# The last layer's window, re-ordered: scores by head pairs, one other use per group, loads ahead of stores

## The reference

```python
def _L3_attn_ref(x, W_qkv, b_qkv, W_proj, b_proj):
    qkv = (x @ W_qkv + b_qkv).reshape(b, n, H, D, 3)
    q, k, v = ...                                   # 4 heads, D = 8
    scores = jnp.einsum('bhnd,bhmd->bhnm', q, k) * scale
    att = jax.nn.softmax(scores, axis=-1)
    out = jnp.einsum('bhnm,bhmd->bhnd', att, v)
    return out @ W_proj + b_proj
def _L3_ffn_ref(x, router_w, router_b, expert_w, expert_b):
    router_probs = jax.nn.softmax(x @ router_w + router_b, axis=-1)
    top_p, top_i = jax.lax.top_k(router_probs, 2)
    top_p = top_p / jnp.sum(top_p, axis=-1, keepdims=True)
    expert_out = jnp.einsum('bnd,edc->bnec', x, expert_w) + expert_b
    return jnp.einsum('bnk,bnkc->bnc', top_p, gathered)
...
t = t + _L3_attn_ref(_ln_t(t), ...)
t = t + _L3_ffn_ref(_ln_t(t), ...)
```

## Time and profile before

| | us |
|---|---|
| three executions | 8492.71, 8477.82, 8460.32 |
| profiled execution: time / span | 8467.15 / 8464.8 |
| PE busy | 6645.8 (79%) |
| DVE busy | 5057.2 (60%) |
| ACT busy | 5212.4 (62%) |
| POOL busy | 2198.2 (26%) |
| DVE peak reductions, 2048 of them | 2445.8, with 825.8 idle ahead of them |
| ACT exponentials of this layer, 4096 of them | 2214.2, with 734.9 idle ahead of them |

### The profile page before, as it was taken

One profiled execution on the slowest core, in us unless ns is written; L12 is line 12 of the kernel. 1 busy time (PEld: TensorE's weight loads), 2 busy tenths in 40 slices (PEclk: granted clock), 3 DMA queues, 4 the chain that ended last, 5 costly groups with the idle time before them and its releaser, 6 DMA issues. The chain is left out here.

```text
span 8464.8 us, 152843 instructions
## 1 busy us (share of the span) xinstructions
PE 6645.8 (79%) x48081; PEld 2768.6 (33%) x48272; DVE 5057.2 (60%) x7798; ACT 5212.4 (62%) x8588; POOL 2198.2 (26%) x3329
## 2 busy tenths in 40 slices
PE   3457888888888888666648888888888888888887
PEld 3223444444444444334432222222222222222222
DVE  5544555555555555423327777777777777777775
ACT  0116777877877787500006776776767767777676
POOL 0021222222222222200012333333333333333333
PEclk7668998899999999855658999999999999999999
DMA  1010000000000000111110000000000000000000
GB/s 70 11 40 9 5 6 6 6 5 6 6 5 6 6 6 5 17 20 20 20 16 5 7 7 9 7 9 7 7 9 7 7 9 7 9 7 7 9 7 7
DMA packets 502054, 92.38 MB, mean 11 GB/s; under 512 B 475742, under 2 KB 501295, under 8 KB 501423
## 3 DMA queue, kind: packets, MB, share of 16 engines
q1 hardware_dynamic: 500399, 86.02, 5.6%
q10 hardware_dynamic: 1152, 0.05, 0.0%
HBM read 52.47 MB, written 33.56 MB: 10 GB/s over the span
## 5 line engine op out<-in xcount | busy, mean ns | idle before, releaser
L2014 DVE TENSOR_REDUCE d_peaks<-d_p_k 128x2 f32<-128x1024 f32 x2048 | 2445.8, 1220 | 825.8 <-PE d_p_k L1865 807.3
L1733 ACT ACTIVATE d_wt<-d_p_s 128x512 f32<-128x512 f32 x4096 | 2214.2, 605 | 734.9 <-PE d_p_s L1837 728.7
L735 ACT ACTIVATE b_sq<-b_p_s 128x1024 f32<-128x1024 f32 (+3 forms) x1536 | 1269.7, 827 | 371.9 <-PE b_p_s L831 364.6
L744 ACT ACTIVATE b_wt<-b_sq 128x1024 f32<-128x1024 f32 (+3 forms) x1536 | 1328.1, 865 | 222.1 <-POOL b_sq L703 222.1
L1837 PE MATMUL d_p_s<-d_qT,d_kT 64*128 64x512 bf16 x4096 | 1278.2, 390 | 215.2 <-ACT d_wt L1733 91.7
L1849 PE MATMUL d_p_o<-d_wt,d_v_pad 128*32 128x512 f32 x8192 | 1135.3, 627 | 0.7 <-ACT d_wt L1733 0.7
L831 PE MATMUL b_p_s<-b_qT,b_kT 128*128 128x512 bf16 (+3 forms) x2881 | 756.2, 362 | 223.7 <-ACT b_sq L735 207.0
L703 POOL TENSOR_SCALAR_AFFINE_SELECT b_sq<-b_sq 128x256 f32<-128x256 f32 x1024 | 422.4, 418 | 1922.3 <-ACT b_sq L735 1922.3
L1865 PE MATMUL d_p_k<-d_kT,d_qT 64*128 64x512 bf16 x4096 | 878.9, 394 | 18.6 <-DVE d_peaks L2014 16.7
L843 PE MATMUL b_p_o<-b_wt,b_v_pad 128*32 128x512 f32 (+3 forms) x6144 | 706.1, 536 | 1.2 <-ACT b_wt L744 1.2
L1837 PEld LDWEIGHTS d_p_s<-d_qT,d_kT 64*128 64x128 bf16 x4096 | 320.2, 95 | 874.6 <-ACT d_wt L1733 391.7
(11 more groups left out here) (278 smaller groups left out, 9201.4 us busy)
## 6 DMA issues: line engine op xcount, KB each, us to landing
w<-in_L_conv_W SPq DMA_DIRECT2D x64, 128.0 KB, 2.1
t<-rows SPq DMA_DIRECT2D x64, 128.0 KB, 1.8
b_x_in<-t SPq DMA_DIRECT2D x64, 128.0 KB, 2.6
t<-b_result SPq DMA_DIRECT2D x64, 128.0 KB, 2.2
c_x_in<-t SPq DMA_DIRECT2D x64, 128.0 KB, 2.7
t<-c_result SPq DMA_DIRECT2D x64, 128.0 KB, 2.7
d_x_in<-t SPq DMA_DIRECT2D x64, 128.0 KB, 3.3
d_x_keep<-t SPq DMA_DIRECT2D x64, 128.0 KB, 3.8
```

Source lines behind the costliest of these rows:

```text
L735: act.activation(sq[:, n % SQ_RING, :, 0:m], p_s[n % 2][:, :, 0:m], ACT.Square).then_inc(squared, 1)
L744: act.activation(wt[:, n % RING, :, 0:m], sq[:, n % SQ_RING, :, 0:m], ACT.Silu, scale=1.0 / D).then_inc(weighed, 1)
L1733: act.activation(wt[:, n % RING, :], tile(n)[:, :], ACT.Exp, scale=SCALE).then_inc(s_used, 1)
L2014: dve.tensor_reduce(peaks[:, m, :], tile(m)[:, :, :], X, ALU.max).then_inc(k_used, 1)
```

## The change

- Two scores of a head pair are issued together (`scores`), on rows 0 to 63 and 64 to 127 of the array, once both banks are free.
- A group is now: pair, peak, other uses, pair, peak, `add_up` of the group before. Tables `S_MISC` and `K_MISC` name the other uses by group; most groups have one.
- The sums are turned in halves, "o0" in group 10 of the own window and "o1" in group 2 of the next one.
- SP issues load, keep, and then the store of image w-2.
- POOL makes prep's squares ahead of `shift_parts` of high; `split` is cut in two, with `shift_parts` of low between them.
- DVE's work is placed anew: routing ends behind m = 29 (before: 24), prep's split starts behind m = 16 (before: 11), the sum of prep's squares stands behind m = 2 (before: 1).
- The loop holds six windows in each turn instead of three. The number of banks and tiles is the same.

```diff
-assert (B - 2 - LOOPED) % 3 == 0
+UNROLL = 6
+assert (B - 2 - LOOPED) % UNROLL == 0
 S_BANKS, K_TILES = 3, 2
 EXPS = 2 * J * H
+GROUPS = EXPS // H
 PAIRS = J * 2 * 2
 RING = 8
-LAG = 3
-
-S_AFTER = {5: ("high",), 11: ("attT",), 13: ("xlT",), 18: ("qkv0",), 19: ("qkv1",), 26: ("xl4T",), 30: ("route",),
-           33: ("experts0", "experts1"), 36: ("experts2", "experts3"), 39: ("low",), 43: ("k0",), 45: ("k1",),
-           47: ("q0",), 49: ("q1",)}
-S_ROLE = {"high": "own", "attT": "prev", "xlT": "prep", "qkv0": "prep", "qkv1": "prep", "xl4T": "prev",
-          "route": "prev", "experts0": "prev", "experts1": "prev", "experts2": "prev", "experts3": "prev",
-          "low": "next", "k0": "prep", "k1": "prep", "q0": "prep", "q1": "prep"}
-K_AFTER = {2: "o", 8: "proj"}
+
+S_MISC = {3: ("xlT",), 4: ("attT",), 5: ("high",), 6: ("qkv0",), 7: ("qkv1",), 9: ("low", "xl4T"), 10: ("route",),
+          11: ("experts0", "experts1"), 12: ("experts2", "experts3"), 13: ("k0",), 14: ("k1",), 15: ("q0", "q1")}
+K_MISC = {2: ("o1",), 5: ("proj",), 10: ("o0",)}
+ROLE = {"xlT": "prep", "attT": "prev", "high": "own", "qkv0": "prep", "qkv1": "prep", "low": "next", "xl4T": "prev",
+        "route": "prev", "experts0": "prev", "experts1": "prev", "experts2": "prev", "experts3": "prev",
+        "k0": "prep", "k1": "prep", "q0": "prep", "q1": "prep", "o0": "own", "o1": "prev", "proj": "prev"}
...
 def s_order(on):
     out = []
-    for n in range(EXPS):
-        if "own" in on:
-            out.append(n)
-        out += [name for name in S_AFTER.get(n, ()) if S_ROLE[name] in on]
+    for a in range(GROUPS):
+        out += [H * a, H * a + 1] if "own" in on else []
+        out += misc(S_MISC, a, on)
+        out += [H * a + 2, H * a + 3] if "own" in on else []
     return out
 
 
 def k_order(on):
     out = []
-    for m in range(PAIRS):
-        if "next" in on:
-            out.append(m)
-        if m in K_AFTER and "prev" in on:
-            out.append(K_AFTER[m])
+    for a in range(GROUPS):
+        out += [2 * a] if "next" in on else []
+        out += misc(K_MISC, a, on)
+        out += [2 * a + 1] if "next" in on else []
     return out
...
+        self.stores = not (isinstance(w, int) and w < 2)
...
-        body(Window(w, w % 3, roles(w)))
-    with eng.Fori(0, (B - 2 - LOOPED) // 3) as k:
-        for d in range(3):
-            body(Window(3 * k + (LOOPED + d), (LOOPED + d) % 3, ALL))
+        body(Window(w, w % UNROLL, roles(w)))
+    with eng.Fori(0, (B - 2 - LOOPED) // UNROLL) as k:
+        for d in range(UNROLL):
+            body(Window(UNROLL * k + (LOOPED + d), (LOOPED + d) % UNROLL, ALL))
     for w in range(B - 2, LAST + 1):
-        body(Window(w, w % 3, roles(w)))
+        body(Window(w, w % UNROLL, roles(w)))
...
-                if "prev" in win.on:
-                    store(win.image("prev"))
                 if "own" in win.on:
                     keep(win.image("own"), win.slot("own"))
+                if win.stores:
+                    store(win.image("prev") - 1)
 
             over_windows(sp, body)
+            store(B - 1)
...
+            def squared(i, step_sem, square_sem, cen, sq):
                 pool.wait_ge(step_sem, 3 * i + 2)
                 pool.tensor_tensor(sq[:, :, :], cen[:, :, :], cen[:, :, :], ALU.mult).then_inc(square_sem, 1)
+
+            def normalise(i, step_sem, var_sem, made_sem, cen, sqs, va, rs, out, free):
                 pool.wait_ge(step_sem, 3 * i + 3)
...
                 pool.wait_ge(split_step, 4 * q + 1)
-                pool.tensor_tensor(rest, qk, both(0), ALU.subtract).then_inc(rest_made, 1)
-                pool.tensor_copy(slot(1, Q), slot(0, Q)).then_inc(spread_made, 1)
-                pool.tensor_copy(slot(4, Q), slot(0, Q)).then_inc(spread_made, 1)
+                pool.tensor_tensor(rest, qk, both(u, 0), ALU.subtract).then_inc(rest_made, 1)
+                pool.tensor_copy(slot(u, 1, Q), slot(u, 0, Q)).then_inc(spread_made, 1)
+                pool.tensor_copy(slot(u, 4, Q), slot(u, 0, Q)).then_inc(spread_made, 1)
+                pool.tensor_copy(slot(u, 2, K), slot(u, 0, K)).then_inc(spread_made, 1)
+
+            def split_second(win):
+                q, u = win.image("prep"), win.slot("prep")
+                rest = left[:, :, :].rearrange("p j (a d) -> p j a d", d=D)
                 pool.wait_ge(split_step, 4 * q + 2)
                 pool.wait_ge(rest_made, 2 * q + 1)
-                pool.tensor_tensor(rest, rest, both(3), ALU.subtract).then_inc(rest_made, 1)
...
             def body(win):
+                q, p = win.image("prep"), win.image("prev")
+                if "prep" in win.on:
+                    squared(q, ln_step, ln_square, centred, square)
                 if "own" in win.on:
                     shift_parts(win.image("own"), win.slot("own"), 1)
...
                 if "prep" in win.on:
-                    split(win)
+                    split_first(win)
                 if "next" in win.on:
                     shift_parts(win.image("next"), win.slot("next"), 0)
+                if "prep" in win.on:
+                    split_second(win)
                 if "prev" in win.on:
                     combine(win)
...
                     act.wait_ge(summed, 16 * i + 8 * (qc + 1))
-                    if qc:
-                        act.wait_ge(k_made, win.k0 - 1)
-                    elif "prev" in win.on:
-                        act.wait_ge(k_made, win.k_done("o"))
+                    act.wait_ge(k_made, win.k0)
...
+                        weigh(H * a)
+                        weigh(H * a + 1)
+                    if "prev" in win.on and a == 1:
+                        copy_o(p, 1)
+                    if "own" in win.on and a == GROUPS // 2 + 1:
+                        copy_o(o, 0)
+                    for name in misc(S_MISC, a, win.on):
+                        copy_misc(name)
+                    if "own" in win.on:
+                        weigh(H * a + 2)
+                        weigh(H * a + 3)
+                    if "prev" in win.on and a == 12:
+                        exp_router()
...
-                def score(n):
+                def scores(n):
                     qc, kb, h = UNITS[n]
-                    rows = slice(64 * (h % 2), 64 * (h % 2) + 64)
-                    bank = seat(n)
-                    pe.matmul(bank[:, :], kT[rows, win.u, h // 2, kb * P:(kb + 1) * P],
-                              qT[rows, win.u, h // 2, qc * HALF:(qc + 1) * HALF], start=True, stop=True).then_inc(s_made, 1)
+                    wait(pe, s_used, win.s_done(n + 1) - S_BANKS)
+                    for r in range(2):
+                        rows = slice(64 * r, 64 * r + 64)
+                        pe.matmul(seat(n + r)[:, :], kT[rows, win.slot("own"), h // 2, kb * P:(kb + 1) * P],
+                                  qT[rows, win.slot("own"), h // 2, qc * HALF:(qc + 1) * HALF],
+                                  start=True, stop=True).then_inc(s_made, 1)
...
+                def turn_o(i, half):
+                    arrived(o_copied, 2 * i + 1 + half)
+                    bank = free_tile(f"o{half}")[:, 0, :]
+                    for j in range(J // 2):
+                        ins = pe.transpose(bank[:, j * P:(j + 1) * P], o_sb[:, half, j * P:(j + 1) * P], ident[:, :])
...
+                for a in range(GROUPS):
                     if "own" in win.on:
-                        score(n)
-                        if n >= LAG + H - 1 and (n - LAG) % H == H - 1:
-                            add_up(o, win.u, (n - LAG) // H)
-                    if "prev" in win.on and n == LAG - 1:
+                        scores(H * a)
+                    if "next" in win.on:
+                        peak(2 * a)
+                    for name in misc(K_MISC, a, win.on) + misc(S_MISC, a, win.on):
+                        use_misc(name)
+                    if "own" in win.on:
+                        scores(H * a + 2)
+                    if "next" in win.on:
+                        peak(2 * a + 1)
+                    if "own" in win.on and a > 0:
+                        add_up(o, win.slot("own"), a - 1)
+                    if "prev" in win.on and a == 0:
                         if "own" not in win.on:
                             pe.wait_ge(s_used, win.s0)
...
+                def scaled():
                     step(dve.reciprocal(col[:, :], col[:, :]))
                     dve.tensor_tensor(mix[:, :, :], mix[:, :, :], mid(col[:, :], ER), ALU.mult).then_inc(mix_made, 1)
...
                 for m in range(PAIRS):
                     if "next" in win.on:
                         peak(m)
-                    if "own" in win.on and m == 0:
-                        dve.wait_ge(k_used, win.k0)
-                        shift_most(o, 1)
+                    if "prev" in win.on:
+                        if m == 4:
+                            attended(p, 1)
+                        if m == 10:
+                            residual()
```

(33 more changed lines are left out.)

203 lines of the change are left out of this document (81 added, 122 removed).

## The result

The changed kernel takes 8645.26 us (median of 4 runs, 8634.67 to 8652.49), the kernel before on the same chip 8477.61 (4 runs). The ratio is 1.0197, with a 95% interval of 1.0174 to 1.0221. The profiled execution has a span of 8650.4 us (8464.8 before) at a mean granted clock of 0.861 (0.878). The forecast was 8536, +58 us; measured are +168. The sign was right, the size was not, and the time lies 5 us above the range.

The account below looks back on a forecast made before the run. No engine is full; time lies in how engines wait for each other. 29.3 us (group 12 to 3) plus 34.1 (groups 3 to 11) gives 63.4 against 62.46, times 62 windows +58 us: 8536, range 8400 to 8640.

Parts of the forecast that it names:

- The load's wait: Top of the window: SP issues the load without waiting for `combine`, so DVE's 2.9 us wait goes.
- the experts' second pair waits for a copy: Groups 11 and 12: the second pair needs banks that a copy must empty, so each group takes 4.9 us.
- the chain through `combine`: Window's top: router's exponential, five reductions, `combine`, squares, reduction 3, "o1"; PE stands 3.7 us, group 3 begins at 29.3.
- groups 3 to 11, put at 34.1 us: Sum of 4 x 3.12, 3.5, 2.6, 7.1, 3.5 and 4.9 us for the groups after the window's top.
- the loop, put at 0: Loop turn: PE's 2.35 us fall into its 3.7 us stand; 0 to 0.4 us a window if POOL stands too.
- I take half: Group 9: the lower clock after PE's 2.85 us wait at "low" costs about 1 us; half counted, 6.65 becoming 7.1.
- Two banks free after the first exponential: 1.07: Steady group: the second pair follows the first by 1.07 us, one trip through ACT; the group stays 2.61 us.
- all terms at their high ends: Upper case of the sum: 29.9 + 34.6 + 0.4 = 64.9 us a window, 8629 us.
- Worse: Rival, chance 0.14: POOL's loop turn lies on the chain and PE is slow after both waits; 64.9 us a window, 8629.
- The exchange is even: Rival, chance 0.15: PE keeps its clock through "low", finds it early at the top; window 62.3 to 62.5 us, about 8475.
- `combine` isn't in the way: Rival, chance 0.15: at "o1" POOL's squares are done by reduction 2's end, PE doesn't stand; window 58.8 us, 8251.
- PE's places count: Rival, chance 0.08: PE sets the round, not ACT's trip; 0.22 us saved in each of 16 groups, 8260 us.

Follow-up runs that it names:

- "low" in time: The changed kernel with low's shift ahead of the first split on DVE and POOL: 8397.11 us, 0.9934 of the kernel before.
- the fastest version: The changed kernel with low's shift first, router's exponential behind group 11, routing closed up, and no common wait of a pair: 8074.77 us, ratio 0.9537.
- The last two experiments: The changed kernel with low's shift first, router's exponential behind group 11, routing closed up: 8154.6 us; the same without the pair's common wait: 8074.77 us.

## Why the prediction was right in sign and too small

Forecast and measured lengths, in the window from 6303.87 to 6369.31 us (65.44), which has no loop turn in it and is one of those with the lower clock behind "o1". T12 is the start of group 12.

| step | forecast | measured |
|---|---|---|
| groups 3, 4, 6, 7 (one small use) | 3.12 each | 3.17, 3.17, 3.18, 3.17 |
| group 5 | 3.5 | 3.39 |
| group 8 (steady) | 2.6 | 2.68 |
| group 9 ("low") | 7.1 | 7.55 |
| group 10 | 3.5 | 3.85 |
| group 11 (experts) | 4.9 | 5.20 |
| T12 to last routing step | 14.2 | 14.5 |
| T12 to squares done | 24.1 | 24.6 |
| T12 to "o1" | 25.8 | 26.2 |
| T12 to group 3 | 29.3 | 30.1 |
| window without a turn | 63.4 | 65.44 |

**Right.** The load's wait goes (SP's order alone shows it), PE waits 2.73 us at "low" (2.85), the experts' second pair waits for a copy, the chain through `combine` sets the next group 3, and pairs gain nothing in a steady group. Where each was isolated, its mechanism held.

**The step that failed** is the size of two terms of the sum: groups 3 to 11, put at 34.1 us, and the loop, put at 0. The path from T12 to group 3 came out right in the mean, 29.45 us in 29 windows where 29.3 was forecast, but partly by luck: "o1" came 0.4 us late in all of them, and the clock, taken as low, was back early in 13 (some 28.7 us there, some 30.1 in the others, of which this window is one). Groups 3 to 11 take 35.36 us in this window and 35.55 in the mean of the 29, 1.4 more than forecast, and the loop adds 0.43. Three causes carry this.

- *The lower clock after "low".* "I take half" was wrong. The sums took 1.93 us (1.78 to 1.94 in all 37 windows from 5500 to 7900 us), and group 10 began at the lower clock as well (a score pair of 0.61 instead of 0.39): +0.45 and +0.35. With "low" in time the sums take 1.06 again.
- *The round of a pair.* "Two banks free after the first exponential: 1.07" became 1.15 in the trace, and a steady group took 2.68. Without the pair's common wait it took 2.61. The forecast counted the common wait as an event of ACT's; but it costs 0.07 us a group by itself. Why, the runs don't show. It is a part of what the groups lost, and of the experts' 0.3 (they take 5.12 us without it). The rest of the experts' 0.3 is not explained: their copies started 2.94 us into the group where 2.77 had been counted.
- *The loop.* Of the turn I took 0 with a bound of 0.4 a window. The two windows with a turn took 67.84 and 67.33 us, the other thirteen 64.97 in the mean: 2.6 for a turn, 0.43 a window. So the high end held. POOL's own turn stands between `combine` and the squares, as the bound had supposed; the trace shows it in POOL's timeline:

```profile
6168.14 0.61 POOL L1651 TENSOR_TENSOR d_square<-d_centred 128x256 f32<-128x256 f32 x1 [2.23 <-issue]
```

The mean window of 65.32 is 1.9 above the forecast; 1.9 x 62 = 119 us, against the 109 by which the median missed. The forecast's "all terms at their high ends" was 64.9. It was too low because the ends of nine groups together had been drawn 0.5 us apart from their middle, as if their errors would cancel; eight of the nine were longer than forecast. Two small slips in the forecast change nothing here: four terms given as 15.9 add up to 15.8, and the rival's window of 58.8 is said to hold the loop's 0.4, but 24.7 + 34.1 is 58.8 without it.

**Not foreseen, and hidden.** The centring's 2.1 us beside `combine` were in no step. They changed where PE waits (before peak 3 instead of at "o1"), and so the waits at "o1" and at the squares came out at a fifth and a third of the forecast, though the chain behind them kept its length. With the common wait taken away the centring took 0.89 us in the mean, and the forecast's waits appeared.

**The rivals.** "Worse" (8629), POOL's loop turn on the chain and PE slow after both waits, describes most of what happened, and the time went 16 us beyond it; but PE was slow after "o1" in 16 of 29 windows only. "The exchange is even" was wrong at "low", where the clock fell in every window. "`combine` isn't in the way" was false here, and true in the fastest version. "PE's places count" is refuted: without the common wait a steady group takes 2.61 us, what it took before the change.

**Open.** SP's order is worth -249 us on the kernel before; that it is worth the same in the changed kernel is assumed, no run took it out there. "low" costs 225 us in the changed kernel and the chain about 170; the pairs' wait costs 80 us once the chain is gone (8154.60 - 8074.77). These don't add to 417, since they overlap, and no run separates them further. No run has the pairs alone or the sums turned in halves alone, so their own prices aren't known. Nor is it known why the clock comes back ahead of "o1" in some windows and not in others.

## What to carry to other kernels

When a wait is removed, follow the chain that then becomes the last to its end, and price every link: here one reordering on a DMA queue was worth 3%, and a regrouping made at the same time cost 417 us, mostly through two new waits, and moving a few lines took them away. Price a new wait of PE with the lower clock behind it in full where a trace of the same kernel shows such a fall: here 2.7 us of waiting cost 1.2 us more, 0.87 in the sums and 0.35 in the next group. A saving in an engine's steady groups is worth nothing while another chain sets the window's end; try it again once that chain is short (0.2 us a window became 1.3 by the times).

## What the runs showed of the hardware

**An operation on DVE stretched by one on POOL.** The centring reads two operands in SBUF. Its mean length by form, 5500 to 8400 us:

```profile
L2049 DVE SCALAR_TENSOR_TENSOR d_centred<-d_total,d_x_in 128x256 f32<-128x256 f32 x45 | 103.3, 2296 | 1.6
```

Before the change it took 424 ns, with SP's order alone 425, with `combine` shortened 442, and 433 in the fastest version, where it stands clear of `combine`. In the window above POOL's first sum started at 6357.86 and by form takes 2.35 us, so it ended near 6360.2; the centring began at 6357.94 and ended at 6360.49, and the 2.55 - 0.42 = 2.13 us that it lost are close to the 2.3 that were left of POOL's operation. The reductions of peaks, which read PSUM, kept their 1.23 us beside `combine`. The Trainium skill, SBUF — State Buffer, section "Who interferes with whom", has this rule: a DVE instruction with two SBUF inputs and a GpSimd instruction that reads SBUF exclude each other, and whichever issues first holds the port for its whole length. The trace agrees within 0.2 us.

**A turn of the loop can stop PE twice.** PE's timeline at a turn of the changed kernel:

```profile
6161.08 0.61 PE L1851 MATMUL d_p_s<-d_qT,d_kT 64*128 64x512 bf16 x2 [2.70 <-issue]
...
6164.23 0.61 PE L1851 MATMUL d_p_s<-d_qT,d_kT 64*128 64x512 bf16 x2 [2.11 <-issue]
```

There are 14 such gaps in seven turns, 2.4 us each. The kernel before with six windows a turn has one in a turn. So has the changed kernel without the pair's common wait, 5500 to 8200 us:

```profile
PE d_p_s L1850 <- issue: 16.9, 7, 2.6
```

The last two experiments, which differ in the common wait alone, have 14 gaps with it and 7 without it, 5500 to 8000 us. So the second gap comes and goes with the common wait, and that is part of what taking it away was worth there. The Trainium skill, Runtime: NRT & Kernel Launch, section "Instruction fetch mechanics", says that a taken branch to a target outside the window held on the engine makes it fetch before it goes on. One gap in a turn fits that, though no view here shows the fetch itself; of a second gap it says nothing, and why the common wait brings one the runs don't tell.
